# Attention scores in two 64-row tiles of TensorE: one half of the partitions per head, two heads per pair of banks

## The reference

```
x = x + 0.5 * ffn(layernorm(x))
q, k, v = split(layernorm(x) @ W_qkv.T + b_qkv)        # 16 heads of 16
scores  = einsum('bqhe,bkhe->bhqk', q, k) / sqrt(16)
scores  = where(key <= query, scores, -inf)
x = x + einsum('bhqk,bkhe->bqhe', softmax(scores), v) @ W_out.T + b_out
x = x + 0.5 * ffn(layernorm(x))
```

## Time and profile before

| | |
|---|---|
| Median of 3 runs | 1588.7 us (1587.25 to 1589.63) |
| Span of the profiled execution | 1575.1 us |
| Mean granted TensorE clock over the span | 0.908 of full speed |
| Softmax stage, from its first memset to the last output | 519.6 to 1118.6 us |
| Busy share of the span: PE, DVE, ACT, POOL | 87%, 65%, 49%, 32% |

### The profile page before, as it was taken

The page is one execution under the profiler, slowest core; times in us unless marked ns, Lnnn a source line. Parts: engine busy times, 40 slices in busy tenths (PEclk is TensorE's granted clock), DMA queues, the critical chain, the costliest instruction groups (busy, mean ns, idle before and its releaser), DMA issues. The chain is left out here.

```text
span 1575.1 us, 31188 instructions
## 1 busy us (share of the span) xinstructions
PE 1364.8 (87%) x8678; PEld 1013.1 (64%) x8709; DVE 1020.5 (65%) x2337; ACT 779.6 (49%) x1949; POOL 497.3 (32%) x651
## 2 busy tenths in 40 slices
PE   2629999899789499999998999999777289998998
PEld 1417888799778255555555555554455168887998
DVE  6583444389867787777776777772385934443787
ACT  2524555433344036666665666666545145554333
POOL 1544333345300201122211112221416543332454
PEclk9658999999989569999998999999886589999999
DMA  5503333322365742223422222200315023333333
GB/s 186 165 0 101 107 107 106 85 64 73 89 256 227 139 63 42 42 43 57 66 44 43 42 42 43 42 2 2 117 53 178 14 88 107 107 107 84 95 111 106
DMA packets 86669, 135.73 MB, mean 86 GB/s; under 512 B 13152, under 2 KB 66336, under 8 KB 83488
## 3 DMA queue, kind: packets, MB, share of 16 engines
q1 hardware_dynamic: 65056, 90.29, 22.0%
q0 software_dynamic: 13056, 35.67, 8.0%
q10 hardware_dynamic: 8448, 8.39, 1.6%
HBM read 81.35 MB, written 52.43 MB: 85 GB/s over the span
## 5 line engine op out<-in xcount | busy, mean ns | idle before, releaser
L1454 DVE TENSOR_REDUCE s_MX<-s_ps_a 128x1 f32<-128x512 f32 (+4 forms) x624 | 368.8, 643 | 134.5 <-PE s_ps_a L1521 132.9
L1428 ACT ACTIVATE s_PR<-s_ps_b 128x512 f32<-128x512 f32 (+3 forms) x768 | 343.8, 491 | 162.4 <-PE s_ps_b L1543 155.3
L1521 PE MATMUL s_ps_a<-s_KO,s_QO 96*128 96x512 f32 (+3 forms) x768 | 286.4, 423 | 23.2 <-DMA s_QO<-qk_scratch 23.2
L1543 PE MATMUL s_ps_b<-s_QO,s_KO 98*128 98x512 f32 (+3 forms) x768 | 267.0, 369 | 7.1 <-issue 3.9
L1397 POOL TENSOR_SCALAR_AFFINE_SELECT s_PR<-s_PR 128x256 f32<-128x256 f32 x256 | 103.4, 406 | 475.2 <-ACT s_PR L1428 474.3
L604 POOL DMA_INDIRECT f_XG<-xn_scratch,f_tok_u x144 | 136.3, 947 | 206.2 <-PE f_ps_x L703 196.4
L1543 PEld LDWEIGHTS s_ps_b<-s_QO,s_KO 98*128 98x128 f32 x768 | 146.7, 194 | 72.4 <-ACT s_PR L1428 54.5
L1521 PEld LDWEIGHTS s_ps_a<-s_KO,s_QO 96*128 96x128 f32 x768 | 152.4, 212 | 28.7 <-DVE s_MX L1454 20.7
L1558 PE MATMUL s_ps_o<-s_PR,s_VG 128*17 128x512 f32 (+3 forms) x1536 | 163.1, 497 | 5.3 <-POOL s_PR L1397 5.3
L816 POOL DMA_INDIRECT f_YG<-y_scratch,f_slots_u x128 | 121.0, 945 | 146.6 <-DVE X L891 86.5
L659 DVE TENSOR_TENSOR f_xl<-f_ps_x,f_xh 128x256 fp32r<-128x256 f32 x144 | 61.2, 425 | 124.0 <-ACT f_xh L629 124.0
(11 more groups left out here) (207 smaller groups left out, 3035.0 us busy)
## 6 DMA issues: line engine op xcount, KB each, us to landing
y_scratch<-f_YS SPq DMA_DIRECT2D x144, 128.0 KB, 1.7
s_KO<-qk_scratch SPq DMA_DIRECT2D x48, 256.0 KB, 6.2
s_QO<-qk_scratch SPq DMA_DIRECT2D x96, 128.0 KB, 6.6
xn_scratch<-f_XN ACTq DMA_DIRECT2D x16, 512.0 KB, 3.2
qk_scratch<-p_QKh SPq DMA_DIRECT2D x32, 256.0 KB, 2.0
qk_scratch<-p_QKl SPq DMA_DIRECT2D x32, 256.0 KB, 2.0
f_stage<-in_w_up SPq DMA_DIRECT2D x20, 352.0 KB, 3.3
X<-in_x SPq DMA_DIRECT2D x4, 1024.0 KB, 9.5
```

The source lines that it names most:

```text
L1428: nc.scalar.activation(PR[:, u // 2 % SLOTS, u % 2, 0:W - lo], ps_b[u % RING][:, lo:W], ACT.Exp, scale=SCALE).then_inc(exp_done, 1)
L1454: nc.vector.tensor_reduce(MX[:, h:h + heads, i, s], ps_a[v % RING][:, 0:heads * keys].rearrange("p (h n) -> p h n", h=heads), AX.X, ALU.ma ...
L1521: last = nc.tensor.matmul(ps_a[v % RING][:, at:at + keys], QO[k][0:R, h, i * P:(i + 1) * P], KO[k][0:R, h % 2, s * W:s * W + keys], start= ...
L1543: nc.tensor.matmul(ps_b[u % RING][:, lo:W], KO[k][0:RM, h % 2, i * P:(i + 1) * P], QO[k][0:RM, h, hf * W + lo:(hf + 1) * W], start=True, s ...
```

## The change

A head's three parts are now stacked with 16 rows each, without the other head's rows: `R` is 48, `RM` 50. The four heads of a group are numbered by half `c` (0, 1) and pair `hp` (0, 1). Half 0 has its operands on partitions 0 to 63, half 1 on 64 to 127 (`TILE` = 64). `QO` shrinks to two heads in the free dimension, and its zeros are gone. `KO`'s ones are written over 32 partitions of both halves before the loads.

Heads now go in pairs. An A unit is (i, s, hp, heads, keys) for both halves: two mask matmuls if it lies on the diagonal, then for each hp one score matmul on each half, into two banks, `ps_a[(2v + c) % 3]`. There are 21 such units (`NA`) and 42 reads by DVE, where there were 39 of each; 128 keys now give two heads to a bank, not four. `b_pair` does the same for B, into `ps_b[(u + c) % 3]`. The rings keep three banks, and the wait stands before the pair: an A pair waits until the first of the two reads of the pair before it is done (`a_read >= NA2*g + 2v + 2 - RING`), a B pair until the first exponential of the pair before it is done (`u + 2 - RING`). `a_done` and `b_done` are two semaphores each, one for each half. SP issues 12 DMAs for a load and 4 for the maximum rows.

```diff
-    PH = 2 * HD
-    R = 3 * PH
+    R = 3 * HD
     RM = R + 2
+    TILE = P // 2
...
-            wide = W // keys
-            starts = range(0, GH, wide)
-            A_UNITS += [(i, s, h, min(wide, GH - h), keys) for h in starts]
+            wide = min(W // keys, 2)
+            A_UNITS += [(i, s, hp, wide, keys) for hp in range(0, 2, wide)]
...
-    LOAD = 9 * 16
-    PLACE = 2 * 16
+    LOAD = 12 * 16
+    PLACE = 4 * 16
...
-            nc.vector.memset(QO[0][0:RM, :, :].bitcast(F32), 0.0).then_inc(zeros[0], 1)
-            nc.vector.memset(KO[0][R:RM, :, :].bitcast(F32), 1.0).then_inc(ones, 1)
+            for k in range(4):
+                for c in range(2):
+                    rows = slice(c * TILE + 32, (c + 1) * TILE)
+                    nc.vector.memset(KO[k][rows, :, :].bitcast(F32), 1.0).then_inc(ones, 1)
             nc.vector.memset(ps_o[:, :], 0.0)
...
-                    if v >= RING or since(g, 1):
-                        pe.wait_ge(a_read, NA * g + v + 1 - RING)
+                    if v >= 1 or since(g, 1):
+                        pe.wait_ge(a_read, NA2 * g + 2 * v + 2 - RING)
...
-                    for h in range(h0, h0 + heads):
-                        at = (h - h0) * keys
-                        last = nc.tensor.matmul(ps_a[v % RING][:, at:at + keys], QO[k][0:R, h, i * P:(i + 1) * P],
-                                                KO[k][0:R, h % 2, s * W:s * W + keys], start=not diagonal,
-                                                stop=True, skip_group_check=True)
-                    last.then_inc(a_done, 1)
+                    for hp in range(hp0, hp0 + heads):
+                        at = (hp - hp0) * keys
+                        for c in range(2):
+                            rows = slice(c * TILE, c * TILE + R)
+                            last = nc.tensor.matmul(banks[c][:, at:at + keys], QO[k][rows, hp, i * P:(i + 1) * P],
+                                                    KO[k][rows, hp, s * W:s * W + keys], start=not diagonal,
+                                                    stop=True, skip_group_check=True)
+                            if hp == hp0 + heads - 1:
+                                last.then_inc(a_done[c], 1)
...
-                if u >= RING or since(g, 1):
-                    pe.wait_ge(exp_done, GH * NB * g + u + 1 - RING)
-                nc.tensor.matmul(ps_b[u % RING][:, lo:W], KO[k][0:RM, h % 2, i * P:(i + 1) * P],
-                                 QO[k][0:RM, h, hf * W + lo:(hf + 1) * W], start=True, stop=True).then_inc(b_done, 1)
+                if u >= 2 or since(g, 1):
+                    pe.wait_ge(exp_done, GH * NB * g + u + 2 - RING)
+                for c in range(2):
+                    rows = slice(c * TILE, c * TILE + RM)
+                    nc.tensor.matmul(ps_b[(u + c) % RING][:, lo:W], KO[k][rows, hp, i * P:(i + 1) * P],
+                                     QO[k][rows, hp, hf * W + lo:(hf + 1) * W],
+                                     start=True, stop=True).then_inc(b_done[c], 1)
```

81 lines of the change are left out of this document (38 added, 43 removed).

## The result

The changed kernel takes 1756.0 us, the median of 4 runs (1750.8 to 1778.2); the kernel before took 1588.0 us in 4 runs beside it (1586.5 to 1589.6). The ratio is 1.1055, with a 95% interval from 1.1023 to 1.1087; it leaves out the run of 1778.2, a slow one. The changed kernel is slower by 168 us, where the forecast was 19 us slower and the range ended at 1660.

A forecast was written before the change was run, and what follows sets the result against it. TensorE's order of work was taken as the bound in steady groups, DVE at the start, ACT at the end. 1575.1 + 9 + 13 - 3 = 1594 us of span, plus 13.6 us around it: 1608 us, range 1568 to 1660.

The forecast's parts named there:

- the term for the clock: Softmax stage's steady groups: the main sum kept them at full clock and added nothing for a fall.
- rival 1: Softmax groups: the clock falls for one to two spells in 15 groups, 16 to 33 us, about 1633 us; chance 22%.
- the two stretches: Parts of a new group without PV, 4.5 and 3.4 us, where pairs stream for only 1.6 and 1.3 us.
- price for a spell: Group steps at half clock: 4.4 us for 3.0, so a spell of 3.4 us costs 1.1.
- The links: Shortest distance between two A pairs, through DVE's read: 1.28 us, 0.1 more on the diagonal; groups together +13 us.
- A pair side by side: TensorE's two half matmuls streaming together: 0.28 us, or 0.33 us where the pair was waited for.
- Rival 2: TensorE's tiles don't run side by side: 4 us a group, 60 over the stage, 1668 us; chance 8%.
- DVE: Reads in a group: 42 for 39, 0.45 us more a group, hidden beside TensorE.
- The start: Softmax stage's start at low clock: group 0's A units +8.1, A(1) +2.7, first load -1; together +9 us.
- The end: Half of group 14 and group 15, paced by ACT and the B link: shorter steps, -3 us.
- The 13.6 us around the span: Whole program: 13.6 us taken as time around the span, added to 1594 us of span.
- Rival 3: Groups paced by TensorE's columns, not the link: 1483 us; a milder form 1568 us; both together 16%.

The follow-up runs named there:

- e15: e2 with the second matmul of each pair cut to 16 columns from group 1 on (B: second step on), all reads and waits kept: 1771.2 us.
- e7: The kernel before with only pass B's score matmuls cut to 64 contracted rows (third product and maximum left out), pass A unchanged: 2110.0 us.
- e6: The changed kernel with query and key rows in DRAM reordered so a load reads contiguous pieces twice as large: 1759.0 us.
- e2: The changed kernel's pairs and waits, with operands of the kernel before (96 or 98 rows), a pair's matmuls one behind the other: 1670.1 us.
- e5: The kernel before with score matmuls cut to the first 66 contracted rows (most of the third product and the maximum left out): 1604.6 us.
- e10: The kernel before without the mask matmuls of pass A, maxima taken over whole blocks: 1555.4 us, 0.981 of before.

## Why the prediction was wrong, step by step

**What failed: the term for the clock.** The sum of 1608 us has the groups at full clock, that is 0 us for a fall of the clock; rival 1 gives it 16 to 33 us. The runs show 126 us in the fifteen groups. The prediction saw the mechanism. It noted that pairs side by side stream for only 1.3 to 1.6 us in stretches of 3.4 to 4.5 us, as little as where the clock had fallen in the last group. It then allowed for the fall in those two stretches alone, one or two spells of 3.4 us in a group, and gave the case 22%. The clock was low for 22.9 us of a group, three to seven times as long as two spells or one. The error is in taking the two stretches as the exception. The steps with a PV in them have less to stream as well: half of the score columns went from all of them, and the waits for the reads are in all of them. The argument "the work done in them is the same as now" counted products, but the array streams columns, and the change's purpose was to halve those. e15 shows that with the same waits this halving is enough, without a tile.

**Its price for a spell was right.** A third of the time at half clock was forecast; the rows give 0.35. With 22.9 us in place of 3.4 to 6.8, the same sum gives 15 x 22.9 x 0.35 = 120 us on top of 1608, 1728 us.

**The links.** 1.28 us was forecast for an A link and 2.98 for a step; the trace has 1.27 and 2.92. The diagonal link is 1.50 and not 1.38: a change of tiling was taken as 0.09, from the change to column tiles, twice on the path less what lies beside other work; with 64-row tiles a change costs 0.2 (e7), and the mask matmuls stand 0.21 us ahead of their scores. A group at full clock was forecast at 34.7 us and comes out at 35.3. Against the 33.7 of before that is 1.6 us more where 0.9 was forecast, 24 us over fifteen groups for the +13 of the sum.

**A pair side by side.** Forecast at the price of about one matmul, 0.28 us and 0.33 where it was waited for. Behind a wait, from 831.00 to 831.34, it is 0.34. Rival 2, tiles that don't run side by side, is refuted by the same rows.

**DVE** has 25.3 us of work in a group for 24.4; +0.45 was forecast and twice that came, hidden beside TensorE in both cases, as DVE waits for TensorE in every step.

**The start.** +8.1 us for group 0's A units, measured +11.1; +2.7 for A(1), measured 11.9 us for 8.5, +3.4. Both have more diagonal pairs than plain ones, and the diagonal link was a term that was too low; that it explains all of the 3 us is not shown. For the load -1 us was forecast and +0.8 came. The load did begin 2 us earlier, as forecast (its first DMA is issued at 528.41, 8.5 us behind the last projection matmul, where before had 10.7), and a memset over 32 rows does take 1.76 us, but from there the first A unit was 15.4 us away for 12.5. The pieces of its source are not the reason (e6). From 540 to 564 us the DMA engines moved 121 GB/s with a share of 1.05 where before had 155 with 1.03; why, stays open.

**The end** was forecast 3 us shorter and is 9.2 longer, with a mean clock of 0.60 between 1250 and 1300 us. The end was worked out at full clock, although the rows of before show the clock falling there. It is the same error as in the first point, but the pairs in tiles are not needed for it: the same stretch (47.3 us at 0.69 in after) took 47.9 us at 0.71 in e2 and 48.2 us at 0.59 in e5, whose regular groups were at 1.00.

**The 13.6 us around the span** are not time around it: the profiled execution of after took 1.8 us more than its span (1752.6 for 1750.8). The term is the distance from a fast execution of before to its median, and the sum still needed it, since it starts from the span of that fast execution.

**Rival 3** decided itself where the prediction said: at the link. Had the clock stayed up in the fifteen groups, 1756 - 126 = 1630 us would have come out by this estimate, still slower than before, so the side of the forecast and its reason hold; the main forecast would still have been 22 us too low, for the links and the start. What broke the range is the clock.

## What to carry to other kernels

Packing matmuls side by side halves the time in which the array streams their columns and changes nothing about the readers behind it. Where those readers set the pace afterwards, first work out what share of each step TensorE will still stream, and expect the clock to go if it is much lower than in the neighbour that keeps it; here that cost five times what the waits themselves did. A kernel that is bound by TensorE at full clock gains more from streaming less that nobody needs (the masks of e10, 2% of the program) than from streaming the same faster. And compare matmuls of exactly 64 rows with 66 before relying on the smaller ones: if only one tile is in use, it has no gain and can lose the clock.
